# Products of zeros in PE's long waits, and the local layer's gate matmuls ahead of its first keys-major scores

## The chip, the cores and the metric

The kernel runs on one core of one Trainium2 chip. Its engines run side by side and meet at semaphores: TensorE (PE, matrix products into PSUM), VectorE (DVE), ScalarE (ACT), GpSimd (POOL) and SyncE (SP), which issues nearly all DMAs. The metric is the device time of one execution in microseconds (us). TensorE's clock is granted by the chip at 2.4 GHz or at 1.2 GHz; the profile shows it as PEclk, 1.00 or 0.50.

## The reference

Two transformer layers with adaptive layer norms over x of shape (2, 512, 256), all in float32:

```
mod = silu(c) @ wmod                       # sa, ca, ga, sb, cb, gb: shift, scale, gate, twice
ga, gb = sign * max(|.|, 0.25)
x = x + ga * attention(layernorm(x) * (1 + ca) + sa)
x = x + gb * ffn(layernorm(x) * (1 + cb) + sb)
```

Layer 0: sliding-window attention (16 heads of 16, a query sees itself and the 64 keys before it), then a mixture of 16 experts (4 chosen) and a shared expert. Layer 1: causal attention with 16 query heads and one key/value head, then a mixture of 8 experts (2 chosen) and a shared expert of width 1024. The gates and shifts of a layer come from `mod` and depend on c alone.

## The kernel before

Every engine has its own program, written out by hand in order; a semaphore wait holds everything behind it on that engine. Products in float32 precision are made of three or more products of high and low parts ("hi", "lo").

**Setup (L505 to 557).** PE computes the first shifts (`shifts(0, j, 7)`), then `norm_transposes(0)`: 16 transposes of the normalized x, for batch 0 from VectorE (`xn`, L1232), for batch 1 from ScalarE (L938).

**Maxima pass (`maxima_pass`, L653).** For each batch b and each of 16 heads PE computes scores in queries-major form (`scores`, L610) from a masked copy of q that ScalarE makes (`mask_q`, L959); VectorE reduces them to negated row maxima `nmx` (`maxima`, L1286). In layer 0 the projections of batch 1 (`project0(1, m)`) stand between the first four heads, and `max_rows(l, b)` (L644) transposes the maxima of a batch, which ScalarE and VectorE split into high and low parts (`max_high`, `max_low`). These are stored to DRAM, where they become two extra rows of q.

**Values pass (`values_pass`, L742).** SyncE loads q (with the maxima rows) and, in layer 0, k of each head from DRAM into four slots (`load_keys_major`, L309); a slot is refilled when its last reader, `keys_major(l, u)` (L679), has passed (`wait_ge(st, u - 3)`). `keys_major` computes the scores in keys-major form in two alternating halves of PSUM, ScalarE exponentiates them (`exponentials`, L1023, semaphore `p`; `keys_major` u waits for `p` u - 1), and after each four heads PE multiplies with V (`values`, L706); VectorE transposes and divides (`outputs`, L1309), GpSimd makes the low part (`out_low`, L431). In layer 0, between `keys_major` 1 and 2, PE computes the remaining shifts (`shifts_rest0`, 8 products of 2 columns) and the gates (`gates(0)`, 8 products of 256 columns in float32, two records each, into banks 6 and 7); PE then waits for the low maxima (`mlo`) and until ScalarE has copied the gates (`gate_taken`, L930), since the value products use the same banks. ScalarE does that copy behind its second exponential (L1043).

**Out-projection, norm, feed-forward.** `out_projection` (L774) ends PE's work of an attention. VectorE multiplies by the gate, adds to x, and takes the statistics (`gated`, L1360, `norm`, L1217), and PE waits for xn in `norm_transposes` (L541). ScalarE and VectorE make the modulated `hF` from the transposes (L946, L1242), PE zeroes the four output banks with `zero` (L812, products of `zeroR` with `maskR`, 512 columns), computes the router's `logits` (L782, 32 records of few columns), and goes into `ffn` (L818), whose first products wait for the high and low parts of h. Between the layers stand `shifts1` and `gates(1)`, then `norm_transposes(2)` and the projections of layer 1 (`project1`).

The functions that the diff touches:

Of the kernel before, what the change touches and what calls it, by code (L numbers as in the profile page):

```python
# [14 lines left out]
B, S, D = 2, 512, 256  # L15
# [46 lines left out]
def build(nc, io, out):  # L62
    ctx = ExitStack()
    with ctx:
# [24 lines left out]
        zeroR = sb("zeroR", [P, P], F32R)  # L89
# [390 lines left out]
        def _(pe):  # L480
# [126 lines left out]

            def scores(l, g, s, b):  # L610
                a = at[l]
                u = 4 * g + s
# [40 lines left out]
            def maxima_pass(l, beside):  # L653

                pe.wait_ge(consts, CONSTS)
                if l == 0:
                    pe.wait_ge(qlo, 4)
                else:
                    pe.wait_ge(v1_taken, 1)
                for b in range(B):  # L660

                    pe.wait_ge(qhi, (4, 6)[b] if l == 0 else 4 * B + 3 * (b + 1))
                    for s in range(SLOTS):
                        scores(l, BQ * b, s, b)
                        for work in beside[b][s]:
                            work()
                    if b:
                        if l:
                            pe.wait_ge(v1_taken, 2)
                        max_rows(l, 0)  # L670
                        if l == 0:
                            pe.wait_ge(qhi, 4 * B)
                    with pe.Fori(BQ * b + 1, BQ * (b + 1)) as g:
                        for s in range(SLOTS):
                            scores(l, g, s, b)
                max_rows(l, 1)


# [61 lines left out]
                        ins.then_inc(y_ps, 1)  # L740

            def values_pass(l):  # L742
                for s in range(2):
                    keys_major(l, s)
                if l == 0:
                    shifts_rest0()
                    gates(0)
                pe.wait_ge(at[l]["mlo"], B)
                if l == 0:
                    pe.wait_ge(gate_taken, 2)  # L750
# [23 lines left out]
            def out_projection(l):  # L774
# [3 lines left out]
                project_out(l, 1, range(OC - 1), False)  # L778
                pe.wait_ge(at[l]["ol"], QUADS)
                project_out(l, 1, range(OC - 1, OC), False)  # L780

            def logits(l):  # L782
                E = EXPERTS[l]
# [115 lines left out]
            ffn(0)  # L899
            shifts1()  # L900
            gates(1)
            norm_transposes(2)

            for m in range(4):
# [12 lines left out]
        def _(act):  # L917
# [119 lines left out]

            def attention(l):
                if l == 0:
                    act.wait_ge(split, 3)  # L1040
                for u in range(UNITS):
                    exponentials(l, u)
                    if l == 0 and u == 1:  # L1043
                        gates(0)

            attention(0)

# [570 lines left out]
```

## Time and profile before

| | us |
|---|---|
| median of 3 runs | 710.63 |
| the runs | 707.0, 710.63, 711.78 |
| the profiled execution | 715.33 |
| its span, first to last instruction | 713.5 |
| mean granted clock of TensorE | 0.955 |
| PE busy | 633.7 (89%) |
| VectorE busy | 389.9 (55%) |
| ScalarE busy | 294.0 (41%) |
| the chain that ended last: share of PE | 71% |
| the same: share of VectorE | 12% |

The times of all the views below are microseconds from the first instruction of that one execution. A timeline row merges like instructions: its start, its duration, engine, source line, operation, tiles and count, and in brackets how long the engine had been idle and who released it. The duration of a matrix product holds the tail of the last one, so the distance between starts is what one costs. A window row gives, for a stretch, the busy time of each engine with its number of instructions, then the granted clock. Work of PE in the two halves of a product in float32 shows as two records.

### The profile page before, as it was taken

How to read it: one execution, taken by the hardware profiler on the slowest of the kernel's cores; microseconds unless marked ns; L12 is line 12 of the kernel's file. 1: busy time of each engine (PE TensorE's matmuls, PEld its weight loads, DVE VectorE, ACT ScalarE, POOL GpSimd, SP SyncE). 2: the span in 40 equal slices, each digit the busy share in tenths (PEclk: the TensorE clock that was granted, in tenths of full speed). 3: DMA queues.
4: the chain of work that ended last, by engine and by line, in shares of the span. 5: the costliest groups of instructions: out<-in, count | busy, mean ns of one | idle time of the engine just before them, and what ended most of it. 6: DMA issues, size and time to landing. Idle time of an engine off the chain costs nothing.

```text
span 713.5 us, 11274 instructions
## 1 busy us (share of the span) xinstructions
PE 633.7 (89%) x3990; PEld 545.0 (76%) x3990; DVE 389.9 (55%) x730; ACT 294.0 (41%) x435; POOL 144.3 (20%) x142
## 2 busy tenths in 40 slices
PE   4989788859899999999999696779987799999995
PEld 3878677757788888888888575667667688888884
DVE  6378144676745544544457779952337633334455
ACT  4466255323443333343331743435660534433331
POOL 5411024403522222222220000001123032222220
PEclk9999799978999999999999999978999699999999
DMA  8444366310011111111100030412221001111101
GB/s 319 112 164 177 93 165 174 98 45 0 24 44 45 53 56 44 44 44 44 44 22 1 4 118 18 136 51 64 76 91 45 0 23 45 44 45 44 44 22 59
DMA packets 27199, 48.92 MB, mean 69 GB/s; under 512 B 4672, under 2 KB 9184, under 8 KB 27168
## 3 DMA queue, kind: packets, MB, share of 16 engines
q1 hardware_dynamic: 26848, 48.38, 22.1%
q8 instruction: 19, 0.31, 0.2%
q10 hardware_dynamic: 320, 0.13, 0.1%
q14 instruction: 12, 0.10, 0.0%
HBM read 36.57 MB, written 11.93 MB: 68 GB/s over the span
## 4 chain that ended last, share of the span: by engine, by line
PE 71%; DVE 12%; ACT 4%; SPq 4%; DMA 4%; issue 3%; POOL 1%; DVEq 0%; ACTq 0%
PE PS L492 33%; PE PS L831 15%; PE PS L700 3%; PE PS L723 3%; PE PS L736 3%; DVE nmx L1299 3%; PE PS L636 2%; DMA qk_slot<-k_scr 2%; PE PS L553 1%; SPq L318 1%; DVE stats L1207 1%; PE PS L789 1%; PE PS L702 1%; DVE xn L1369 1%; DVE x L1373 1%
## 5 line engine op out<-in xcount | busy, mean ns | idle before, releaser
L492 PE MATMUL PS<-h_hi,wqkv_hi 128*128 128x512 f32 x352 | 122.3, 407 | 4.0 <-POOL wqkv_hi L456 2.1
L1080 ACT ACTIVATE qk_hi<-xn 128x512 fp32r<-128x512 f32 x82 | 51.8, 632 | 178.0 <-DVE xn L1481 138.8
L492 PE MATMUL PS<-h_hi,wqkv_lo 128*128 128x512 f32 x336 | 113.7, 396 | 0.0
L1478 DVE TENSOR_TENSOR pr<-pr,PS 128x512 f32<-128x512 f32 x60 | 41.3, 688 | 86.8 <-PE PS L492 86.8
L492 PEld LDWEIGHTS PS<-h_hi,wqkv_hi 128*128 128x128 f32 x352 | 68.6, 195 | 19.4 <-POOL wqkv_hi L456 2.3
L1483 DVE TENSOR_TENSOR qk_lo<-xn,qk_hi 128x512 fp32r<-128x512 f32 x74 | 51.2, 692 | 52.7 <-ACT qk_hi L1080 52.7
L492 PE MATMUL PS<-h_lo,wqkv_hi 128*128 128x512 f32 x184 | 74.7, 406 | 0.0
L492 PEld LDWEIGHTS PS<-h_hi,wqkv_lo 128*128 128x128 f32 x336 | 63.5, 189 | 13.5 <-issue 0.3
L1076 ACT ACTIVATE pr<-PS 128x512 f32<-128x512 f32 x82 | 48.8, 596 | 43.0 <-PE PS L492 42.8
L831 PE MATMUL PS<-wqkv_hi,qk_hi 128*128 128x256 f32 x336 | 62.1, 284 | 3.3 <-POOL qk_lo L462 1.7
L456 POOL TENSOR_TENSOR wqkv_hi<-fw_raw,wqkv_hi 128x768 fp32r<-128x768 f32 x21 | 40.9, 1948 | 113.3 <-ACT wqkv_hi L1069 113.3
L492 PE MATMUL PS<-h_lo,wqkv_lo 128*128 128x512 f32 x160 | 62.8, 392 | 0.0
L456 POOL TENSOR_TENSOR wqkv_lo<-fw_raw,wqkv_lo 128x768 fp32r<-128x768 f32 x20 | 37.8, 1889 | 117.4 <-ACT wqkv_lo L1069 117.4
L831 PE MATMUL PS<-wqkv_lo,qk_hi 128*128 128x256 f32 x320 | 58.8, 283 | 1.6 <-DVE qk_lo L1483 1.5
L831 PEld LDWEIGHTS PS<-wqkv_hi,qk_hi 128*128 128x128 f32 x336 | 53.8, 188 | 8.3 <-POOL qk_lo L462 2.7
L1299 DVE TENSOR_REDUCE nmx<-PS 128x512 f32 (+4 forms) x96 | 53.8, 637 | 5.4 <-PE PS L639 5.3
L831 PEld LDWEIGHTS PS<-wqkv_lo,qk_hi 128*128 128x128 f32 x320 | 51.4, 188 | 5.5 <-DVE qk_lo L1483 1.7
L636 PE MATMUL PS<-qk_hi,q_masked 128*128 128x256 f32 (+2 forms) x128 | 40.0, 377 | 12.9 <-DVE nmx L1299 9.2
L963 ACT ACTIVATE q_masked<-qk_hi,headmask 128x512 fp32r (+1 forms) x64 | 43.1, 716 | 14.8 <-PE PS L639 12.5
L1314 DVE STREAM_TRANSPOSE o_parts<-PS 128x512 f32<-128x512 f32 x16 | 11.5, 717 | 67.7 <-PE PS L723 67.7
L831 PE MATMUL PS<-wqkv_hi,qk_lo 128*128 128x256 f32 x168 | 47.3, 281 | 0.0
L435 POOL TENSOR_TENSOR h_lo<-o_parts,h_hi 128x512 fp32r<-128x512 f32 x8 | 10.3, 1282 | 179.6 <-DVE h_hi L1327 179.6
(209 smaller groups left out, 1346.3 us busy)
## 6 DMA issues: line engine op xcount, KB each, us to landing
fw_raw<-in_ffn SPq DMA_DIRECT2D x41, 384.0 KB, 3.0
qk_slot<-q_scr SPq DMA_DIRECT2D x64, 132.0 KB
q_scr<-qk_hi SPq DMA_DIRECT2D x16, 256.0 KB
q_scr<-qk_lo SPq DMA_DIRECT2D x16, 256.0 KB
qk_slot<-k_scr SPq DMA_DIRECT2D x64, 64.0 KB
wmod<-in_wmod SPq DMA_DIRECT2D x1, 1536.0 KB, 13.4
x<-in_x SPq DMA_DIRECT2D x2, 512.0 KB, 4.2
wmod<-in_wmod SPq DMA_DIRECT2D x1, 1024.0 KB, 9.5
```

Of the source, the lines that this page charges most:

```text
L456: nc.gpsimd.tensor_tensor(fwR[s][1], fw[s][:, :], fwR[s][0].bitcast(F32), ALU.subtract)\
L492: ins = nc.tensor.matmul(dst, left(a, c), right(b, c), start=n == 0, stop=n == total - 1)
L636: nc.tensor.matmul(PS[:, bank, col:col + WIDTH1[qt]], qm[s][:, qt * P:(qt + 1) * P], qkR[0][:, 2, 0:WIDTH1[qt]], start=True, stop=True)
L700: nc.tensor.matmul(PS[:, bank, col:col + n], k1[:, b, kb * P:(kb + 1) * P], qk[s][:, kb * P:S], start=True, stop=True)
L723: ins = nc.tensor.matmul(PS[s * VW:(s + 1) * VW, O_BANK[g % 2], kb * P:kb * P + n], v, probs[l][slot][:, col:col + n], start=kb == 0, stop ...
L831: ins = nc.tensor.matmul(PS[:, 2 * b + t // 2, (t % 2) * D:(t % 2 + 1) * D], hidR[b][a][:, t * P:(t + 1) * P], fwR[s][w][:, 2 * D:], start ...
L963: nc.scalar.activation(qm[s][:, :], qkR[0][:, bass.ds(head // 2, 1), :].rearrange("p m t -> p (m t)").bitcast(F32), ACT.Copy, scale=headma ...
L1076: nc.scalar.activation(gact[b], PS[:, 4, :], ACT.Silu).then_inc(f["silu"], 1)
L1080: nc.scalar.activation(hidR[b][0], hid[b], ACT.Copy).then_inc(f["hi"], 1)
L1299: nc.vector.tensor_reduce(nmx[:, bass.ds(NT * u + qt, k)], PS[:, 3 * h + bank, 0:k * w].rearrange("p (t k) -> p t k", k=w), X, ALU.max, ne ...
L1478: tt(hid[b] if half is None else gu[b], gact[b], PS[:, 5, :], ALU.mult).then_inc(f["gu"], 1)
L1483: tt(hidR[b][1], hid[b], hidR[b][0].bitcast(F32), ALU.subtract).then_inc(f["lo"], 1)
```

## The change

It adds a helper that multiplies zeros into a PSUM bank that nothing reads, and calls it in seven places of PE's program: before the first scores of batch 1 in each layer (8 products in layer 0, 9 in layer 1, each behind a wait for the bank to be free), before the last `max_rows` of layer 1 (7), at the start of layer 1's values pass (10), at the end of each `out_projection` (30), and between `gates(1)` and `norm_transposes(2)` (7). In layer 0's values pass it moves `shifts_rest0` and `gates(0)` ahead of the first two `keys_major`, and on ScalarE it moves the copy of the gates ahead of the first exponential.

```diff
--- before.py
+++ after.py
@@ -607,6 +607,11 @@
 
 
 
+            def filler(count, bank):
+
+                for _ in range(count):
+                    nc.tensor.matmul(PS[:, bank, :], zeroR[:, :], maskR[:, 0:S], start=True, stop=True)
+
             def scores(l, g, s, b):
                 a = at[l]
                 u = 4 * g + s
@@ -659,6 +664,12 @@
                     pe.wait_ge(v1_taken, 1)
                 for b in range(B):
 
+                    if b and l == 0:
+                        pe.wait_ge(v_taken, 2)
+                        filler(8, 4)
+                    elif b:
+                        pe.wait_ge(qF_ready, 6)
+                        filler(9, 7)
                     pe.wait_ge(qhi, (4, 6)[b] if l == 0 else 4 * B + 3 * (b + 1))
                     for s in range(SLOTS):
                         scores(l, BQ * b, s, b)
@@ -673,6 +684,8 @@
                     with pe.Fori(BQ * b + 1, BQ * (b + 1)) as g:
                         for s in range(SLOTS):
                             scores(l, g, s, b)
+                if l:
+                    filler(7, 7)
                 max_rows(l, 1)
 
 
@@ -740,11 +753,13 @@
                         ins.then_inc(y_ps, 1)
 
             def values_pass(l):
-                for s in range(2):
-                    keys_major(l, s)
                 if l == 0:
                     shifts_rest0()
                     gates(0)
+                else:
+                    filler(10, 7)
+                for s in range(2):
+                    keys_major(l, s)
                 pe.wait_ge(at[l]["mlo"], B)
                 if l == 0:
                     pe.wait_ge(gate_taken, 2)
@@ -778,6 +793,7 @@
                 project_out(l, 1, range(OC - 1), False)
                 pe.wait_ge(at[l]["ol"], QUADS)
                 project_out(l, 1, range(OC - 1, OC), False)
+                filler(30, 7)
 
             def logits(l):
                 E = EXPERTS[l]
@@ -899,6 +915,7 @@
             ffn(0)
             shifts1()
             gates(1)
+            filler(7, 4)
             norm_transposes(2)
 
             for m in range(4):
@@ -1037,11 +1054,10 @@
 
             def attention(l):
                 if l == 0:
+                    gates(0)
                     act.wait_ge(split, 3)
                 for u in range(UNITS):
                     exponentials(l, u)
-                    if l == 0 and u == 1:
-                        gates(0)
 
             attention(0)
 
```

## Rows read from the trace of the kernel before

**Rows 1.** Waits of PE, whole span: us in total, times, longest us

```profile
PE PS L553 <- DVE xn L1232: 18.1, 3, 7.9
...
PE PS L636 <- ACT q_masked L963: 2.5, 1, 2.5
```

**Rows 2.** Timeline of PE, 155 to 165: start us, us, line [idle before <-releaser]

```profile
155.79 1.97 PE L553 MATMUL PS<-ident,xn 128*128 128x128 f32 x8 [7.89 <-DVE xn L1232]
...
159.12 2.05 PE L815 MATMUL PS<-maskR,zeroR 128*128 128x512 f32 x4
160.97 3.84 PE L789 MATMUL PS<-wg,hF 128*128 128x16 f32 x32
```

**Rows 3.** Timeline of PE, 376 to 430, between the layers

```profile
386.20 3.63 PE L500 MATMUL PS<-sc,wmod 128*128 128x2 f32 x32
389.70 5.39 PE L536 MATMUL PS<-wmod,hF 128*128 128x256 f32 x16
397.44 1.09 PE L553 MATMUL PS<-ident,xn 128*128 128x128 f32 x8 [2.36 <-DVE xn L1232]
```

**Rows 4.** Windows: length; PE, PEld, DVE, ACT, POOL busy; PEclk, DMA share, GB/s

```profile
52.30:55.60 3.30, 3.29 (x14) 3.30 (x15) 1.33 (x3) 2.79 (x5) 0.00 (x0) 0.50 0.49 138
76.10:86.30 10.20, 9.68 (x33) 8.78 (x34) 0.34 (x2) 2.90 (x3) 0.00 (x0) 0.50 0.38 99
151.20:161.20 10.00, 5.41 (x22) 5.02 (x23) 6.95 (x25) 4.54 (x8) 0.00 (x0) 0.50 0.01 2
472.10:485.50 13.40, 12.69 (x54) 10.92 (x56) 3.05 (x4) 8.60 (x7) 0.00 (x0) 0.50 0.21 59
554.00:560.60 6.60, 3.34 (x17) 3.34 (x17) 4.23 (x16) 2.56 (x5) 0.00 (x0) 0.50 0.00 0
560.80:564.00 3.20, 3.20 (x27) 3.02 (x26) 2.01 (x4) 3.15 (x6) 0.00 (x0) 1.00 0.00 0
```

**Rows 5.** Timeline of PE, 134 to 138, zero products at the high clock

```profile
137.19 0.63 PE L815 MATMUL PS<-maskR,zeroR 128*128 128x512 f32 x2
```

**Rows 6.** Timeline of PE, 46 to 62, batch change of the local maxima pass

```profile
52.31 0.66 PE L623 MATMUL PS<-maskR,identR 128*128 128x384 f32 x1 [2.04 <-ACT q_masked L963]
```

**Rows 7.** Timeline of PE, 464 to 492, start of the causal values pass

```profile
471.27 0.30 PE L650 MATMUL PS<-ident,nmx 128*64 128x128 f32 x1 [2.01 <-DVE nmx L1299]
...
484.09 1.07 PE L723 MATMUL PS<-pr,V 128*32 128x512 f32 x2
...
487.13 0.50 PE L700 MATMUL PS<-qk_slot,k 128*128 128x512 f32 x1
```

**Rows 8.** Timeline of PE, 70 to 98, start of the local values pass

```profile
75.06 0.44 PE L691 MATMUL PS<-maskR,identR 128*128 128x384 f32 x1 [1.05 <-DMA qk_slot<-k_scr]
...
78.23 3.46 PE L500 MATMUL PS<-sc,wmod 128*128 128x2 f32 x16
81.55 6.04 PE L536 MATMUL PS<-wmod,hF 128*128 128x256 f32 x16
88.81 0.41 PE L691 MATMUL PS<-maskR,identR 128*128 128x384 f32 x1 [1.22 <-issue]
...
95.61 0.44 PE L691 MATMUL PS<-maskR,identR 128*128 128x384 f32 x1 [0.68 <-DMA qk_slot<-k_scr]
```

**Rows 9.** Timeline of ScalarE, 66 to 95

```profile
76.18 1.28 ACT L1030 ACT_TABLE_LOAD   x1 [1.86 <-PE PS L692]
77.47 0.81 ACT L1030 ACTIVATE pr<-PS 128x768 f32<-128x768 f32 x1
...
87.62 1.08 ACT L930 ACTIVATE gate<-PS 128x512 f32<-128x512 f32 x2 [8.35 <-PE PS L536]
```

**Rows 10.** Timeline of ScalarE, 144 to 176

```profile
159.91 1.43 ACT L946 ACTIVATE hF<-PS,modT 128x512 f32<-128x512 f32 x2
```

**Rows 11.** Timeline of ScalarE, 464 to 492

```profile
473.14 1.28 ACT L1036 ACT_TABLE_LOAD   x1 [1.27 <-DVE mxT_lo L1306]
474.44 2.37 ACT L1036 ACTIVATE pr<-PS 128x1280 f32<-128x1280 f32 x2
```

## The prediction

> **What bounds the kernel now.** I read the waits of TensorE (PE) first. Its largest wait by far is for the normalized x: 18.1 us in three waits, the longest 7.9 [rows 1]. The first of them takes 7.89 us [rows 2], the one between the layers 2.36 [rows 3], which leaves 7.9 for the last. I then cut the granted clock into stretches [rows 4]. Around each long wait the clock falls from 2.4 to 1.2 GHz (1.00 to 0.50) and stays low well into the work that follows: 3.3 us after the batch change of the first maxima pass, 10.2 us at the start of the local values pass, 10.0 us around the first of the long normalization waits, 13.4 us at the start of the causal values pass, 6.6 us around the last. PE carries 9.7 us of records in the second stretch and 12.7 in the fourth, so there the low clock costs time on the path; in the third only 5.4 of 10.0 us are work. The timelines of PE and ScalarE (ACT) then tell which of this work ends last [rows 5 to 11].
>
> **The price of a filler.** Four products of zeros of this shape (128x512) take from 159.12 to 160.97, 0.46 us each at the low clock [rows 2]; half of it, 0.235 with rounding up, is the price at the high one, where two of them last 0.63 with the tail of the second [rows 5]. The diff's counts come to 8 x 0.235 = 1.9 us, 9: 2.1, 7: 1.6, 10: 2.35, 30: 7.05. The waits they stand in are 2.04 (8, first maxima pass, [rows 6]), 2.5 (9, [rows 1]), 2.01 (7 before the last row of maxima, [rows 7]), 2.36 (7 before the third normalization, [rows 3]) and 7.89 and 7.9 (30 each). All but the ten fit, with 0.1 to 0.9 us to spare, and cost nothing. If the cover were gone each would cost its whole length; at the low clock the 30 would take 13.8 us. Do zeros hold the clock? The clock is low through 3.3 us of transposes and rises at 161.2, right behind the four zero products of 159.12 [rows 2, 4]. I take it that they count.
>
> **Part by part.** The sum is made in the profiled execution (715.33 us, span 713.5).
>
> (a) Eight fillers in the local maxima pass. PE works at 1.2 GHz from 52.31 to 55.6 [rows 4, 6]; at 2.4 that is 1.6 us less. But ScalarE is busy 2.79 of these 3.30 us, with the masks and the q and k parts that PE and VectorE need next, and behind them VectorE's reductions set the pace; I take 0.45, near the lower end. Ends: 0 and 1.6.
>
> (b) The moved shifts and gates. Now: PE comes free at 74.0, waits 1.05 us for the first query/key slot, does two keys-major scores, then shifts (3.3 us) and gates (6.0), ends at 87.6 and starts the third score at 88.8 [rows 8]. After: shifts start at 74.0. In the second layer the same kind of chain runs without a wait before it: 32 shift records in 3.50 us at 2.4 GHz, and 16 gate records in 5.39, in which the clock is low for a part [rows 3]. So 16 x 0.11 = 1.75 and 5.2: gates end at G = 74.0 + 6.95 = 80.95, 6.65 us earlier. Ends: gates all at 2.4 (3.4 us), or shifts 3.46 and gates 6.8, all at 1.2 (G = 84.3). What follows G gets later, since it loses what it did before. ScalarE copies the gates (1.08), waits for the first score (G + 1.1), loads its exponential table (1.28) and takes 0.81 us for each exponential [rows 9]: the third score starts at G + 3.3 and the fourth at G + 4.15, where before it was G + 1.2. SyncE, which had refilled slots 0 and 1 in the shadow of the gates, now issues these loads after the first scores, so two of the pass's 28 refills fall into it. A slot's refill takes 5.0 us: the fourth score ended at 90.6 (88.81 plus two scores of 0.9) and the same slot's next started at 95.61, waiting for a DMA [rows 8]. So that score now starts at G + 5.1 + 5.0 = G + 10.1 = 91.05, not 95.61: 4.5 us gained. From there on the pass repeats. VectorE's shift copy and gate steps come earlier too, ahead of its first output block, and nobody waits for them; GpSimd's queue has nothing in it. Ends: 1.2 (G = 84.3) to 6.2.
>
> (c) Thirty fillers behind the first out-projection. At 2.4 GHz eight transposes take 0.93 us instead of 1.77 [rows 2, 3]. From 155.79: transposes to 157.65, zeros to 158.6, first half of the logits (16 x 0.115; 32 take 3.84 with a tail) to 160.4; the second half waits for ScalarE's hF, which will end 0.95 earlier than its 161.34 [rows 10], so also at 160.4; with a tail of 0.15 they end at 162.35 instead of 164.81 [rows 2], 2.5 us. The logits are tiny products and the clock can fall within them, as it now does right behind them; 0.3 off: 2.2. The router's VectorE chain starts from there and all moves along. Ends: 0.9 (hF's gain alone) and 3.5.
>
> (d) The same 30 in the second layer, the same working: 2.2.
>
> (e) Seven fillers before the third normalization, nine at the batch change of the second maxima pass: the clock is high in both places as it is. 0.
>
> (f) Causal values pass. Seven fillers keep the clock up over the 2.01 us wait. Ten more delay the first score from 471.4 to 473.75, and with it the table load, which waits for that score (473.14 now, [rows 11]): load at 474.95, first exponential to 477.45, third score at 477.6. From then one score per exponential (1.2 us each, [rows 11]), the sixth ends at 482.5. The value products last from 484.09 to 487.13 with the rise at 485.5 [rows 4, 7]: 1.6 us at the high clock and 1.4 at the low, so 2.3 all at the high. The next score starts at 484.85 instead of 487.13. Gain 2.3. Where an execution of before had not fallen here, the ten fillers cost 1.9 instead.
>
> Sum: 0.45 + 4.5 + 2.2 + 2.2 + 2.3 = 11.65, the profiled execution would take 703.7. It lies 4.7 us above the median (710.63) and the three runs spread over 4.8. The chance falls of the clock, (a) and (f), can be such a spread: I give (f) only 0.8 against the median, the odds of 6 to 4 between 2.3 and -1.9 rounded up a little. 710.6 - 10.1 = **700.5 us**.
>
> **Rivals.**
> 1. The clock still falls in the causal pass. With the fillers there is now a gap of 1.6 us between the second and third score, where ScalarE loads its table. If it falls there, or if it mostly had not fallen before, (f) is -1.9: 703.2 us. For it: a fall at 472 behind 2 us of idling. Chance 0.15.
> 2. Transposes do not hold the clock. After the 30 fillers a rest of 0.8 us and 1.9 us of transposes follow; if the clock falls there, zeros and logits run at 1.2 and (c) and (d) keep 0.9 each: 703.1 us. Against it: in the last normalization the clock rose at 560.7, right behind 3.3 us that held hardly anything but transposes [rows 4]. Chance 0.08. The Trainium skill, page "TensorE: Matmul & The Clock Gate", section "Part 4: PE-mode transpose", says that transposes do not count as busy for the clock; by that rule this rival would be the forecast, and the trace speaks against it.
> 3. The moved gates run all at 1.2 GHz, behind shifts that give the clock no reason to stay up, and the refills pile up: (b) 1.2, total 703.8 us. Chance 0.10.
> 4. Zeros do not hold the clock: slower. It falls 3.3 us into each 30 as it does now [rows 2, 4], the other 16 take 0.46, and PE is 10.7 us behind the out-projection free instead of 7.9: 2.8 us late, twice. In the causal pass two fillers take 0.235, eight 0.46, and the first exponential comes 4.3 us late. 5.6 + 4.3 - 4.5 of (b) = 5.4 us slower, 716.0 us. The point from which it is slower than before: (b) gains under 9.9 us, which its rows exclude to exceed; only the first assumption decides. Against it: the rise behind the zeros [rows 2, 4]. Chance 0.05.
> The moved code is certain to run; that it does not do what it says has no chance of its own.
>
> **How the numbers follow.** Forecast 0.55, own range 696 to 704. Rivals 0.38, and 0.07 for mixtures of small losses, 704 to 709. The range that leaves out 2 in 10 is 695.5 to 707. A measurement of this kernel tells 1% (7.1 us) from no change: faster means under 703.5. That is most of the forecast (0.51), half of rivals 1 and 2 (0.12) and 0.04 of rival 3, some 0.68 in all; slower by 1% (over 717.7) is the upper half of rival 4, 0.03, and a tail of mishaps, 0.02; the rest, 0.27, is within 1%.
>
> **What would show it.** Clock at 1.00 from the first out-projection's end through the transposes, and 8 of them in 0.93 us; third local score 2 us or more behind the gates; gates in about 5.2 us; first causal exponential near 2 us later than now against the last maxima, but the seventh score 2.3 earlier; fillers ending ahead of the event they wait with. Wrong would be: a clock of 0.50 within the fillers, or refill waits on the first eight slots that grow beyond 5 us.

## The result and the profile after

The changed kernel takes **702.51 us** in the median of 15 runs (699.03 to 707.37), the kernel before on the same chip 710.95 in 15 runs (707.0 to 715.1). The ratio is **0.9898, 95% interval 0.9874 to 0.9922**: 7.3 us less by the ratio (5.5 to 9.0), 8.4 by the medians, where 10.1 were forecast. The forecast of 700.5 is 2.0 us too low, inside its range. The mean granted clock of TensorE in the profiled executions rises from 0.955 to 0.983.

The profiled execution of the changed kernel took 702.60 us, that of before 715.33. That difference, 12.7, is not the change's worth: 715.33 lies above all the 15 runs that the kernel before was given beside the changed one. The head of the page after:

```profile
span 700.8 us, 11475 instructions
...
PE 642.4 (92%) x4091; PEld 550.0 (78%) x4091; DVE 390.1 (56%) x730; ACT 293.7 (42%) x435; POOL 144.3 (21%) x142
```

PE is busy for 8.7 us more, in a span that is 12.7 shorter, because the records of the zeros count as busy. VectorE, ScalarE and GpSimd do what they did. Next the waits of PE (us in total, times, longest). The wait for `xn` that led the list [rows 1] is down from 18.1 us to 2.5: the zeros now stand in it.

```profile
PE PS L553 <- DVE xn L1248: 2.5, 3, 0.9
```

Windows of the changed kernel, columns as in [rows 4], whose stretches they answer: the batch change of the first maxima pass, the start of the local values pass, the first normalization, the logits behind it, the start of the causal values pass, the second long normalization.

```profile
50.20:55.60 5.40, 5.25 (x34) 4.46 (x33) 3.42 (x7) 5.14 (x10) 0.00 (x0) 1.00 0.33 92
75.80:79.00 3.20, 3.20 (x9) 2.55 (x8) 0.05 (x1) 0.00 (x0) 0.00 (x0) 0.50 0.54 161
143.30:157.40 14.10, 13.20 (x80) 11.02 (x79) 11.18 (x37) 5.71 (x10) 0.00 (x0) 1.00 0.00 0
157.80:161.00 3.20, 3.20 (x10) 2.62 (x10) 2.17 (x9) 1.59 (x2) 0.00 (x0) 0.50 0.00 0
464.80:477.20 12.40, 11.76 (x92) 9.38 (x92) 3.24 (x4) 8.65 (x8) 0.00 (x0) 1.00 0.25 73
539.40:553.40 14.00, 13.10 (x79) 10.92 (x78) 11.07 (x37) 5.94 (x11) 0.00 (x0) 1.00 0.01 2
```

The clock is at 2.4 GHz in four of the six, and each of the four holds work that was at 1.2 before. In the local values pass it still falls, for 3.4 us where it had been 10.2.

### The profile page after: what moved, and what is told of

It reads as the page before. It is cut to its first block, busy times and chain, and to the rows that moved or that the text cites. A ratio compares the mean times of both kernels' runs of the same rounds, so it can differ in the third digit from the quotient of the medians.

```text
span 700.8 us, 11475 instructions
## 1 busy us (share of the span) xinstructions
PE 642.4 (92%) x4091; PEld 550.0 (78%) x4091; DVE 390.1 (56%) x730; ACT 293.7 (42%) x435; POOL 144.3 (21%) x142
## 4 chain that ended last, share of the span: by engine, by line
PE 73%; DVE 13%; ACT 6%; DMA 3%; issue 3%; POOL 1%; SPq 1%; DVEq 0%; ACTq 0%
PE PS L492 33%; PE PS L847 16%; PE PS L736 4%; PE PS L749 3%; DVE nmx L1315 3%; PE PS L713 3%; PE PS L641 2%; PE PS L628 2%; DMA qk_slot<-k_scr 2%; PE PS L630 1%; PE PS L704 1%; ACT q_masked L980 1%; DMA w_raw<-in_wqkv 1%; DVE x L1389 1%; DVE xn L1385 1%
## 5 line engine op out<-in xcount | busy, mean ns | idle before, releaser
L492 PE MATMUL PS<-h_hi,wqkv_hi 128*128 128x512 f32 x352 | 121.8, 405 | 4.0 <-POOL wqkv_hi L456 2.1
L492 PE MATMUL PS<-h_hi,wqkv_lo 128*128 128x512 f32 x336 | 113.6, 396 | 0.0
L492 PEld LDWEIGHTS PS<-h_hi,wqkv_hi 128*128 128x128 f32 x352 | 67.9, 193 | 19.2 <-POOL wqkv_hi L456 2.3
L492 PEld LDWEIGHTS PS<-h_hi,wqkv_lo 128*128 128x128 f32 x336 | 63.4, 189 | 13.4 <-issue 0.3
L492 PE MATMUL PS<-h_lo,wqkv_hi 128*128 128x512 f32 x184 | 73.7, 400 | 0.0
L492 PE MATMUL PS<-h_lo,wqkv_lo 128*128 128x512 f32 x160 | 62.8, 393 | 0.0
```

Of the source, the lines that this page charges most:

```text
L492: ins = nc.tensor.matmul(dst, left(a, c), right(b, c), start=n == 0, stop=n == total - 1)
```

## Where the time went, stretch by stretch

The table gives the time between starts of PE's rows in one profiled execution of each kernel, in us. "Maxima row" is the transposition of the last maxima of a pass (L650 before, L655 after), "T" the transposes of a long normalization, "ffn" the first product of the feed-forward (L492), "down" its first down product. The kernels below "changed" are those of the experiments.

| kernel | start to local maxima row | to 3rd score | to 8th score | maxima row to T 1 | T 1 to ffn | ffn to T 2 | causal maxima row to 7th score | T 3 to ffn | ffn to down |
|---|---|---|---|---|---|---|---|---|---|
| before | 73.71 | 15.10 | 21.90 | 82.08 | 8.87 | 232.78 | 15.86 | 8.82 | 8.19 |
| changed | 73.43 | 10.65 | 17.68 | 77.98 | 6.71 | 232.78 | 12.38 | 6.80 | 7.29 |
| changed, second profile | 73.09 | 10.66 | 17.42 | 79.42 | 6.56 | 234.26 | 12.39 | 6.56 | 7.54 |
| only the new order | 73.88 | 10.65 | 16.66 | 75.88 | 8.76 | 232.75 | 11.89 | 8.81 | 8.15 |
| only the zeros | 73.50 | 14.94 | 21.77 | 79.78 | 6.56 | 234.26 | 12.39 | 6.57 | 7.55 |
| changed without the ten | 71.76 | 10.66 | 17.81 | 78.37 | 7.04 | 234.86 | 15.90 | 6.56 | 7.54 |
| changed without the thirties | 73.69 | 10.65 | 17.81 | 75.35 | 8.91 | 232.78 | 12.37 | 8.80 | 8.24 |
| only the thirties | 75.21 | 10.46 | 17.74 | 77.45 | 7.74 | 232.75 | 15.87 | 6.57 | 7.54 |
| new order and thirties | 74.13 | 10.65 | 16.94 | 76.82 | 6.56 | 234.26 | 11.97 | 6.56 | 7.53 |
| narrow zeros | 75.02 | 12.32 | 19.40 | 84.22 | 9.02 | 232.78 | 12.39 | 8.82 | 8.28 |
| eight behind the scores | 75.00 | 12.29 | 19.11 | 77.76 | 6.56 | 234.25 | 11.87 | 6.56 | 7.55 |
| gates between | 73.48 | 10.02 | 17.18 | 75.67 | 7.64 | 232.86 | 12.38 | 7.61 | 8.03 |
| combined | 72.31 | 9.47 | 16.29 | 74.31 | 6.86 | 234.28 | 10.59 | 6.57 | 7.54 |
| combined, second profile | 75.04 | 9.32 | 16.51 | 75.25 | 7.74 | 232.80 | 10.59 | 6.56 | 7.54 |

From before to changed the stretches that don't overlap give 0.3 (start), 4.1 (local values pass), 2.2 (T 1 to ffn), 3.5 (causal values pass), 2.0 and 0.9 (around the second router): 13.0 of gains, against 12.7 in the spans; the rest of the passes takes 0.2 back. Most columns take only a few distinct values, with the clock falling or not and with how long it stays low. Much of what separates two executions of one kernel goes with that, and not all: in the 15 runs of the changed kernel, those with a mean clock of 0.986 took 699.0 to 700.7 and those with 0.974 to 0.976 took 704.8 to 706.5, but the longest, 707.37, had 0.981. So one trace tells the mechanism, and the timed runs tell the worth.

## The experiments

All compute the whole reference. The ratio is each kernel's to the kernel before on the same chip. The changed kernel was compared by itself (before: mean 710.9); e1 to e4, e6 to e9 and g1 to g4 each shared a chip and its runs of before (means 711.7, 710.2 and 711.6 us). Behind ± stands the standard error of the mean.

| kernel | median us | mean us | ratio, 95% interval |
|---|---|---|---|
| changed | 702.51 | 702.90 ± 0.66 | 0.9898, 0.9874 to 0.9922 |
| e1 only the new order | 708.97 | 709.27 ± 0.73 | 0.9997, 0.9959 to 1.0035 |
| e2 only the zeros | 704.08 | 704.57 ± 0.53 | 0.9924, 0.9894 to 0.9954 |
| e3 changed without the ten | 705.86 | 705.48 ± 0.72 | 0.9949, 0.9915 to 0.9983 |
| e4 changed without the thirties | 706.99 | 707.12 ± 0.60 | 0.9970, 0.9936 to 1.0004 |
| e6 narrow zeros | 722.4 | one run | |
| e7 eight behind the scores | 703.61 | 703.53 ± 0.50 | 0.9921, 0.9888 to 0.9953 |
| e8 gates between | 701.43 | 701.48 ± 0.47 | 0.9903, 0.9865 to 0.9942 |
| e9 combined | 701.13 | 700.21 ± 0.84 | 0.9903, 0.9866 to 0.9939 |
| g1 changed again | 701.25 | 702.14 ± 1.18 | 0.9856, 0.9813 to 0.9899 |
| g2 only the thirties | 708.33 | 706.95 ± 0.96 | 0.9933, 0.9895 to 0.9970 |
| g3 new order and thirties | 703.95 | 704.05 ± 0.68 | 0.9893, 0.9855 to 0.9931 |
| g4 combined again | 699.53 | 699.89 ± 0.64 | 0.9833, 0.9795 to 0.9870 |

Two kernels stand in the table twice. The changed one has 0.9898 and 0.9856, the combined one 0.9903 and 0.9833: the same kernel differs by 3 and by 5 us from one chip to the next. Differences of 2 or 3 us between kernels of different chips are within that scatter.

### The two halves of the change

**Only the new order** (all calls of `filler` taken out of the changed kernel):

```diff
-                filler(30, 7)
...
-            filler(7, 4)
...
                 if l == 0:
                     shifts_rest0()
                     gates(0)
-                else:
-                    filler(10, 7)
```

> Only the moved shifts and gates, none of the zero products. Theory (my sum, (b)): gates end about 6.9 us behind the last maxima row instead of 13.9, and 4.5 us are gained against before: ratio 0.9937, 706.5 us. The two long normalization waits are as before, with a granted clock of 0.50 at the transposes (8 in 1.77 us). Rival (refills eat it, or gates all at 1.2 GHz): 1.2 us gained, ratio 0.998. Rival (the order does it all): 7.3 us, ratio 0.990.

**Only the zeros** (the order of before on PE and ScalarE, all calls of `filler` kept):

```diff
-                if l == 0:
-                    shifts_rest0()
-                    gates(0)
-                else:
+                if l:
                     filler(10, 7)
                 for s in range(2):
                     keys_major(l, s)
+                if l == 0:
+                    shifts_rest0()
+                    gates(0)
```

> All the zero products, but shifts and gates where they were. Theory: what the order does not give, some 4 us at the two normalizations (2.2 each) and 0 to 3.5 in the causal pass, depending on whether an execution of before had fallen there: in all 4 to 5 us, ratio 0.994. Rival (zeros are worth nothing in the median, the profiled execution of before was only an unlucky one): ratio 1.00. Rival (they do it all): 0.990.

The zeros alone give most of it, 0.9924. The order alone can't be told from nothing by its ratio; by the means on that chip it is 2.4 us faster. Yet its trace shows third and eighth score as early as in the changed kernel (10.65 and 16.66 behind the maxima row), 4.5 and 5.2 us ahead of the profiled execution of before. The mechanism is there and most of the time isn't. Either the pass takes back later what it gained, or the execution of before with which they are compared was an unlucky one.

### The groups of zeros

**Without the ten** (the `filler(10, 7)` at the start of the causal values pass taken out):

```diff
                 if l == 0:
                     shifts_rest0()
                     gates(0)
-                else:
-                    filler(10, 7)
```

> The changed kernel without the ten zero products at the start of the causal values pass. Theory A (my (f)): ScalarE's table load waits for the first score, so the ten cost 1.9 us wherever the clock would not have fallen: this kernel is up to 1.9 us faster than the changed one when the clock stays up, and 2 to 3.5 slower when it falls. Theory B (from the changed kernel's trace): the load stands behind the DMA issues at 466.65, so the first exponential comes only 0.5 us earlier than in the changed kernel, and the idle gap between second and third score grows to about 2.1 us; time within 1 us of the changed kernel's where the clock holds.

**Without the thirties:**

```diff
                 project_out(l, 1, range(OC - 1, OC), False)
-                filler(30, 7)
```

> The changed kernel without the two times thirty zero products. Theory: loses 2.2 us at each of the two long normalizations, 4.4 us slower than the changed kernel, near 707 us, ratio to before 0.995; the clock is at 0.50 at the transposes, 8 of them in 1.77 us, and the first product of the feed-forward stands 8.9 us behind the end of the wait as before, where the changed kernel has 6.7. Rival (the wait of the transposes or hF sets the pace, whatever the clock): no loss, ratio 0.990.

Without the ten the kernel is 2.6 us slower than the changed one by the means, 3.6 by the ratios, and 1.9 if each mean is first taken against the mean of before on its own chip; the intervals of the two ratios overlap. Its trace shows where the time goes. PE's rows at the start of the causal values pass, without the ten:

```profile
465.87 0.30 PE L655 MATMUL PS<-ident,nmx 128*64 128x128 f32 x1 [0.33 <-DVE nmx L1313]
...
470.42 0.76 PE L713 MATMUL PS<-qk_slot,k 128*128 128x512 f32 x1 [2.11 <-ACT pr L1051]
...
481.77 0.50 PE L713 MATMUL PS<-qk_slot,k 128*128 128x512 f32 x1
```

The same of the changed kernel:

```profile
462.60 1.84 PE L613 MATMUL PS<-maskR,zeroR 128*128 128x512 f32 x7
464.77 0.30 PE L655 MATMUL PS<-ident,nmx 128*64 128x128 f32 x1 [0.33 <-DVE nmx L1315]
464.83 2.57 PE L613 MATMUL PS<-maskR,zeroR 128*128 128x512 f32 x10
467.24 0.39 PE L713 MATMUL PS<-qk_slot,k 128*128 128x512 f32 x1
...
469.84 0.48 PE L713 MATMUL PS<-qk_slot,k 128*128 128x512 f32 x1 [0.34 <-ACT pr L1053]
...
477.15 0.50 PE L713 MATMUL PS<-qk_slot,k 128*128 128x512 f32 x1
```

The ten take the place of the wait between the second and the third score: 0.34 us of it are left instead of 2.11. With the wait the clock fell and the seventh score came 15.90 us behind the maxima row; with the zeros 12.38. In the five traces without the ten it fell every time, but not alike. In three (before, this one, only the thirties) it stayed low for 10.2 to 13.7 us, and the seventh score came at 15.86 to 15.90. In two (only the new order, new order and thirties) it fell 0.1 us behind the maxima row or less and was back after 3.4 us, ahead of the third score; there the seventh came at 11.89 and 11.97. Windows of the kernel with only the new order, whose maxima row stands at 465.36:

```profile
465.50:468.50 3.00, 3.00 (x12) 2.81 (x12) 2.43 (x4) 1.50 (x2) 0.00 (x0) 0.50 0.11 30
469.00:475.00 6.00, 5.16 (x40) 4.67 (x42) 0.31 (x1) 5.35 (x5) 0.00 (x0) 1.00 0.30 86
```

Four of the five, all but this one, also lack the seven zeros ahead of the maxima row, and in those four the fall begins within 0.8 us of that row. In the seven traces with ten or eight zeros there it never fell.

Without the thirties 4.2 us are lost by the means and 5.1 by the ratios, and 3.5 by means taken against before on each chip; T 1 to ffn and T 3 to ffn are back at 8.91 and 8.80.

### Do busy records hold the clock?

**Narrow zeros.** Each 30 of 512 columns become 90 of 32 columns.

```diff
-                filler(30, 7)
+                for _ in range(90):
+                    nc.tensor.matmul(PS[:, 7, 0:32], zeroR[:, :], maskR[:, 0:32], start=True, stop=True)
```

> The changed kernel with each run of 30 products of 512 columns replaced by 90 products of zeros of 32 columns, about the same time of busy instructions (PE near 6 us busy at 2.4 GHz). Theory (columns streamed hold the clock, not instructions): the clock falls to 0.50 within or behind them, transposes again take 1.77 us per 8, and the first feed-forward product comes 8.8 us behind the transposes instead of 6.7. Rival (any PE instruction holds it): clock 1.00 through the transposes, 6.7 us.

PE's rows and two windows of this kernel:

```profile
143.95 15.45 PE L797 MATMUL PS<-maskR,zeroR 128*128 128x32 f32 x90
159.24 1.97 PE L553 MATMUL PS<-ident,xn 128*128 128x128 f32 x8
```

```profile
144.00:147.50 3.50, 3.50 (x34) 3.50 (x33) 3.43 (x12) 0.00 (x0) 0.00 (x0) 1.00 0.00 0
148.20:158.00 9.80, 9.80 (x48) 9.80 (x47) 3.35 (x17) 2.08 (x4) 0.00 (x0) 0.50 0.00 0
```

PE is busy for every microsecond of both windows, and the clock falls all the same. At the high clock 34 records take 3.5 us (0.10 each), at the low one 48 take 9.8 (0.20). Even at 0.10 each the ninety would have taken 9.3 us, not the 6 that had been expected, and so more than their cover of 7.9. At the low clock they outgrew it by far: the transposes start 15.3 us behind the first of them, and run at the low clock too, 1.97 us for eight. The second layer does the same, and this single run took 722.4 us. Thirty products of 512 columns over 7.2 us held the clock, ninety of 32 columns did not. An engine that is shown busy is not by that alone one that keeps its clock.

### The place of the zeros in the causal pass

**Eight behind the first two scores** instead of ten ahead of them:

```diff
-                else:
-                    filler(10, 7)
                 for s in range(2):
                     keys_major(l, s)
+                if l:
+                    filler(8, 7)
```

> Changed kernel, but in the causal pass 8 zero products behind the first two scores instead of 10 ahead of them. Theory B (the table load does not wait for the first score): from the last maxima row to the seventh score 11.9 us instead of 12.4, as the kernel with the order alone showed by luck; the clock stays at 1.00 in every execution; median 0.5 us under the changed kernel, ratio 0.989. Theory A (it waits): 1.9 us faster. Rival: the clock falls all the same (the wait before the last row ends it): 15.9 us and a ratio near 0.994.

ScalarE in this kernel, and then in the changed one:

```profile
469.26 1.28 ACT L1053 ACT_TABLE_LOAD   x1 [1.27 <-DVE mxT_lo L1322]
470.56 2.37 ACT L1053 ACTIVATE pr<-PS 128x1280 f32<-128x1280 f32 x2
```

```profile
466.02 0.59 ACTq L256 DMA_DIRECT2D q_scr<-mxT_lo  x1
466.65 1.28 ACT L1053 ACT_TABLE_LOAD   x1 [1.27 <-DVE mxT_lo L1322]
468.46 2.37 ACT L1053 ACTIVATE pr<-PS 128x1280 f32<-128x1280 f32 x2 [0.53 <-PE PS L715]
```

The maxima rows start at 467.38 and 464.77, so the load comes 1.88 us behind both, though the first score stands 0.11 behind the maxima row in the one and 2.47 in the other. In the changed kernel the load even starts before the first score does (467.24). It stands behind ScalarE's DMA issues, not behind the score. In the local pass it is otherwise: the load of before starts at 76.18, when the first score has ended at 76.10 [rows 8, 9], and in the kernel with the gates between, whose first score ends at 76.64, ScalarE stands idle between the DMA issue and the load:

```profile
74.78 0.60 ACTq L256 DMA_DIRECT2D q_scr<-mxT_lo  x1
76.72 1.28 ACT L1048 ACT_TABLE_LOAD   x1 [2.62 <-PE PS L705]
```

In the local program two waits stand ahead of that exponential, in the causal one a single one; no run tests whether this decides it. In the causal pass ten zeros ahead of the scores therefore delay the first exponential by 0.5 us only (3.69 against 3.18 behind the maxima row), which the seventh score shows too, 12.38 against 11.87. The timed runs don't tell the two places apart: 0.9921 against 0.9898, intervals overlapping.

### The order by itself, against the thirties

**Only the thirties** is the kernel before with a `filler(30, 7)` at the end of `out_projection` and nothing else:

```diff
                 project_out(l, 1, range(OC - 1, OC), False)
+                filler(30, 7)
```

> The kernel before with nothing but the two times thirty zero products. Theory: 2.2 us at each of the two long waits (8.8 to 6.6 from transposes to the feed-forward's first product), plus 0.7 behind the second (8.2 to 7.5), less what a fall of the clock near 181 us takes back (1.5): 3.5 to 5 us, ratio 0.994. Rival (the order does more than the zeros): under 2 us, 0.998.

**New order and thirties** is the changed kernel without the small groups:

```diff
-                    if b and l == 0:
-                        pe.wait_ge(v_taken, 2)
-                        filler(8, 4)
-                    elif b:
-                        pe.wait_ge(qF_ready, 6)
-                        filler(9, 7)
...
-                if l:
-                    filler(7, 7)
...
-                else:
-                    filler(10, 7)
...
-            filler(7, 4)
```

> Moved shifts and gates with the two times thirty, none of the 8, 9, 7, 10, 7. Against the run with the thirties alone it shows the order, against the changed kernel the small groups. Theory X (the traces): the order gives 4 us, as the stretch from the last local maxima row to the transposes is 77 us where it was 81; ratio 0.988, and the small groups nothing but the causal 1 to 2. Theory Y (the medians so far): the order gives 2, the small groups 2.5 us, ratio 0.992: the DMA-bound pass takes back what was gained up to the eighth score.

**Changed again**, unaltered, for the same chip:

> The changed kernel once more, on the chip of the three below. Ratio to before 0.988 to 0.990; the reference for the other three.

By the ratios: the thirties alone 4.8 us, the order on top of them 2.8, the small groups on top of both 2.6; by the means of this chip 4.7, 2.9 and 1.9. The first is clear of the noise. For the order and for the small groups the intervals of the ratios overlap. The changed kernel itself came out at 0.9856, better than the 0.988 to 0.990 expected of it. The old order's local values pass, in the kernel with only the thirties (PE, then two windows):

```profile
75.21 0.30 PE L655 MATMUL PS<-ident,nmx 128*64 128x128 f32 x1 [1.22 <-DVE nmx L1299]
...
77.34 1.86 PE L500 MATMUL PS<-sc,wmod 128*128 128x2 f32 x16
79.07 5.39 PE L536 MATMUL PS<-wmod,hF 128*128 128x256 f32 x16
85.67 0.42 PE L696 MATMUL PS<-maskR,identR 128*128 128x384 f32 x1 [1.22 <-issue]
...
92.95 0.45 PE L696 MATMUL PS<-maskR,identR 128*128 128x384 f32 x1 [1.15 <-DMA qk_slot<-k_scr]
```

```profile
75.30:78.90 3.60, 3.43 (x28) 3.26 (x28) 0.28 (x1) 1.96 (x3) 0.00 (x0) 1.00 0.78 191
79.10:82.30 3.20, 3.20 (x9) 2.57 (x10) 0.34 (x2) 0.90 (x2) 0.00 (x0) 0.54 0.49 116
```

These rows show that the old order is not always late. Here it had its shifts at the high clock (1.86 us where [rows 8] have 3.46) and a low stretch of 3.4 us, not 10.2; its first two scores also waited only 0.2 us for their slots, where those of before waited 1.6 and those with only the zeros 1.3. Its third score comes 10.46 us behind the maxima row and its eighth 17.74, as early as in the new order. The 15.10 and 21.90 of the profiled execution of before, which came up again with only the zeros (14.94, 21.77), are the old order with a low stretch of 10.2 us. The new order has a bad draw too, 12.3 and 19.1 to 19.4 in two of its traces, but a smaller one.

The table gives the order's worth once more, by averages over traces. From the maxima row to T 1 the three traces of the old order take 79.8 us and seven of the new one (the narrow zeros left out, which delay T 1 themselves) 77.4, which is 2.4 less. From the eighth score to T 1 it is 59.3 and 59.7. So little of the gain is taken back later, and most of the forecast's excess comes from the one execution of before.

### A version with both repaired

**Gates between**: the shifts stay ahead, the first two scores come next, then the gates; ScalarE copies them behind its second exponential as before.

```diff
                 if l == 0:
                     shifts_rest0()
-                    gates(0)
                 else:
                     filler(10, 7)
                 for s in range(2):
                     keys_major(l, s)
+                if l == 0:
+                    gates(0)
```

> Changed kernel with the local layer's order: shifts, first two scores, gates, third score; ScalarE's gate copy behind its second exponential as before. Theory (the moved gates keep two refills and two exponentials out of their shadow, and the pass lives on its DMAs, so a part of the 4.2 us gained up to the eighth score is given back): the third score starts as early as in the changed kernel (10.5 us behind the last maxima row), the eighth 16.7 to 17.2 us behind it instead of 17.7, and the whole stretch to the transposes is 1 to 2 us shorter; ratio 0.987. Rival (refills are hidden by latency anyway): same as the changed kernel, 0.990. Rival (scores at 1.2 GHz and the gates all at it): 1 us slower.

The third score came 10.02 us behind the maxima row, the eighth 17.18 and T 1 75.67, where seven traces of the new order have 77.4 on average: as the theory had it, in one trace. The timed runs don't confirm it. The ratio is 0.9903, where 0.987 was expected and the changed kernel has 0.9898 and 0.9856. Some of it went elsewhere, at least in the trace: behind both long waits the clock was low for 6.8 us, and T to ffn took 7.64 and 7.61.

**Combined**: the shifts go ahead of the last local maxima row, into a wait of 1.2 us; the gates stand between the second and third score; in the causal pass two zeros stand behind the first two scores, and ScalarE makes its exponential table load early, with an exponential of a tile of two columns, ahead of the last split of the maxima.

```diff
                 if l:
                     filler(7, 7)
+                else:
+                    shifts_rest0()
                 max_rows(l, 1)
...
             mask_rest(1, 1)
+            nc.scalar.activation(bqs[:, :], bqs[:, :], ACT.Exp).then_inc(act_order, 1)
             max_high(1, 1)
...
-                if l == 0:
-                    shifts_rest0()
-                    gates(0)
-                else:
-                    filler(10, 7)
                 for s in range(2):
                     keys_major(l, s)
+                if l == 0:
+                    gates(0)
+                else:
+                    filler(2, 7)
```

> The version the readings point to: shifts_rest0 ahead of the last maxima row of the local layer (in a wait of 1.22 us), first two scores, then gates as in the run before; in the causal pass the exponential table is loaded by an exponential of two columns ahead of the last maxima row, and two zero products behind the first two scores instead of ten ahead. The other zero products stay. Theory: 0.8 us from the shifts, 1 to 2 from the order, 1.8 in the causal pass: 3.5 to 4.5 us under the changed kernel, ratio 0.984. Rival (the DMA-bound local pass takes back what is gained before it): only the causal 1.8, 0.987. Rival (too few zeros in the causal pass, the clock falls): 0.990.

Its trace has the earliest scores of all (9.47 and 16.29 behind the maxima row, the seventh causal one 10.59), and the clock held in the causal pass with two zeros. The ratio, 0.9903, is no better than the changed kernel's, and 0.984 had been expected; the mean, 700.21, is 2.7 us under that of the changed kernel, which ran on another chip.

And the same kernel once more, beside the changed one:

> The combined version once more, beside the changed kernel on one chip. Theory: 2.5 to 3.5 us under it (its trace: 1.8 in the causal pass, 1.1 ahead of the gates, 0.4 to the transposes), ratio 0.985. Rival: no difference that can be measured, 0.989.

The start of the local values pass in that second run of it, and ScalarE at the start of its causal pass:

```profile
73.31 1.86 PE L500 MATMUL PS<-sc,wmod 128*128 128x2 f32 x16
75.04 0.28 PE L655 MATMUL PS<-ident,nmx 128*64 128x128 f32 x1
...
78.62 4.52 PE L536 MATMUL PS<-wmod,hF 128*128 128x256 f32 x16
84.36 0.41 PE L706 MATMUL PS<-maskR,identR 128*128 128x384 f32 x1 [1.22 <-issue]
...
91.55 0.45 PE L706 MATMUL PS<-maskR,identR 128*128 128x384 f32 x1 [1.07 <-DMA qk_slot<-k_scr]
```

```profile
465.05 0.60 ACTq L256 DMA_DIRECT2D q_scr<-mxT_lo  x1
465.70 2.37 ACT L1054 ACTIVATE pr<-PS 128x1280 f32<-128x1280 f32 x2 [1.28 <-PE PS L717]
```

The exponential stands right behind the DMA issues with no table load between, and the seventh causal score comes 10.59 us behind the maxima row instead of 12.38; third and eighth local score come 1.3 and 0.9 us earlier than in the changed kernel run beside it (its maxima row stands behind the shifts, which puts up to 0.5 us of them into the first column). Together that is 2 to 3 us in the traces. The clock gives part of it back elsewhere (T 1 to ffn 7.74 against 6.56 there). The timed runs show 0.9833 against 0.9856 on the same chip, with overlapping intervals. It has the lowest mean of its chip in both comparisons and beats the kernel before clearly; that it beats the changed one is likely by the traces and not shown by the times.

## Why the prediction was right, and which of its terms were not

**Zeros hold the clock: right.** PE's rows behind the first out-projection of the changed kernel:

```profile
143.35 7.16 PE L613 MATMUL PS<-maskR,zeroR 128*128 128x512 f32 x30
151.41 1.09 PE L553 MATMUL PS<-ident,xn 128*128 128x128 f32 x8 [0.90 <-DVE xn L1248]
...
154.22 4.06 PE L805 MATMUL PS<-wg,hF 128*128 128x16 f32 x32
158.12 0.77 PE L492 MATMUL PS<-h_hi,wqkv_hi 128*128 128x512 f32 x1
```

Thirty take 7.16 us with a tail, 0.239 each against the 0.235 of the sum, and eight transposes 0.93 as worked out; the clock is 1.00 from 143.3 to 157.4. Rival 4, the slower outcome, has fallen.

**(c) and (d), the thirties: right.** 2.2 each were forecast; T 1 to ffn is 2.16 shorter and T 3 to ffn 2.02. The timed runs give 3.5 to 5.1 us for both, against 4.4. There is a detail that the step named as a risk: the clock falls again in the logits or right behind them (157.7 here). Where it kept up through the logits, T to ffn is 6.56, another 0.15 to 0.24 less. In some traces it also falls later, in the feed-forward. Two windows around that point, in the kernel with only the zeros:

```profile
160.00:181.00 21.00, 16.59 (x84) 12.91 (x84) 17.53 (x24) 7.10 (x11) 11.67 (x4) 1.00 0.00 1
181.60:184.80 3.20, 3.20 (x8) 2.53 (x9) 2.59 (x7) 0.38 (x1) 1.07 (x1) 0.50 0.41 123
```

Behind a wait of 2.11 us for GpSimd's high parts of the weights the clock falls for 3.4 us, and ffn to T 2 takes 234.26 instead of 232.78. The changed kernel has that wait too (2.13, at 179.83 in the trace shown) and had no fall there. So 1.5 us of the first layer's gain are given back in some executions: the four traces with 6.56 all have 234.25 or 234.26. An earlier fall does not rule out the later one. Without the ten, the clock was low in the logits and again behind that wait, and ffn to T 2 took 234.86:

```profile
155.90:162.50 6.60, 6.60 (x22) 5.44 (x22) 4.74 (x17) 2.19 (x3) 0.00 (x0) 0.51 0.00 0
180.00:183.00 3.00, 3.00 (x9) 2.32 (x8) 2.09 (x7) 0.60 (x1) 0.57 (x1) 0.50 0.41 131
```

The wait is in all fourteen traces, the fall behind it in six: in the three that had no fall between T 1 and it, and in three (this one, new order and thirties, the first combined one) that had. In the second layer there is no such wait, and instead ffn to down came 0.65 to 0.90 earlier, which no step had counted.

**(b), the moved gates: the mechanism right, the term mis-sized.** The step said: gates end at G = 6.95 us behind the point where PE comes free, third score at G + 3.3, eighth at 91.05. The trace:

```profile
73.43 0.30 PE L655 MATMUL PS<-ident,nmx 128*64 128x128 f32 x1 [1.22 <-DVE nmx L1309]
73.56 1.88 PE L500 MATMUL PS<-sc,wmod 128*128 128x2 f32 x16
75.31 5.39 PE L536 MATMUL PS<-wmod,hF 128*128 128x256 f32 x16
80.34 0.53 PE L704 MATMUL PS<-maskR,identR 128*128 128x384 f32 x1
...
84.08 0.41 PE L704 MATMUL PS<-maskR,identR 128*128 128x384 f32 x1 [1.81 <-ACT pr L1047]
...
91.11 0.44 PE L704 MATMUL PS<-maskR,identR 128*128 128x384 f32 x1 [0.91 <-DMA qk_slot<-k_scr]
```

ScalarE copies the gates at 80.73, loads its table at 81.83 and begins the exponentials at 83.13, [rows 9] with the order turned round. Gates to 80.34, 6.8 behind 73.56; third score at G + 3.7; eighth at 91.11, 10.8 behind G. Every event came within 0.7 us of the step, and the refill is again what the eighth score waits for (0.91). But the term, 4.5, was a difference against one execution of before, and that had a low stretch of 10.2 us. The runs give 0.2 (order alone), 1.9 (changed against only the zeros) and 2.8 us (on top of the thirties) by the ratios, and 2.4, 0.9 and 2.9 by means taken against before on each chip: about 2 in the middle, with no single one well clear of the noise. The traces, averaged, give 2.4. The step had called only the falls in (a) and (f) a matter of chance, though (b) rests on one as much. That is the step that failed. The pass behind it scatters as well: from the eighth score to T 1 it took between 57.5 and 62.0 us (64.8 with the narrow zeros), with no relation to the order.

**(f), the causal pass: a premise wrong, a term too small.** The step held the table load to be waiting for the first score, as it does in the local pass (76.18 against 76.10). Here it doesn't (466.65 against the first score's 467.24). So the ten delay the first exponential by 0.5 us and not 1.9; against an execution with a long fall the gain is 3.5 us and not 2.3, and against one with a short early fall it is -0.5. An execution without the ten and without a fall, which the step priced at -1.9, is in no trace. With a long fall in three of five traces without the ten, an estimate is 0.6 x 3.5 - 0.4 x 0.5 = 1.9 us, where 0.8 had been counted. The runs: 1.9 to 3.6 for the ten alone, 1.9 to 2.6 for all small groups together. Rival 1 priced this term at -1.9: its gap of 1.6 us between the second and third score is 0.34, and the clock held in all traces with the ten.

**(a) and (e): small, as said.** With the eight zeros the clock is 1.00 at the first batch change in the trace above (the first of the windows), and they end at 52.28, 0.15 ahead of the scores that follow. Those start at 52.43 where they started at 52.31 [rows 6], so the eight fill their wait to the end and leave nothing to spare.

From the start to the last local maxima row it is 73.62 us in the mean over eight traces with them (71.76 to 75.02; the two combined ones left out, which have shifts in it) and 74.23 over four without (73.71 to 75.21): 0.6 us within a scatter of 3, against 0.45 forecast, and so neither shown nor contradicted.

**Rivals 2 and 3.** Rival 3 had the moved gates all at 1.2 GHz; the low stretch in them is 3.4 us in most traces and 6.8 in two, and the third score was 12.3 behind the maxima row at the worst. Its price, 1.2 for (b), is nevertheless nearer to what the order is worth than the 4.5, for another reason. Rival 2 had the clock fall in the transposes: in the changed kernel, from 151.41 to 153.1, it is 1.00. The Trainium skill, page "TensorE: Matmul & The Clock Gate", section "Part 4: PE-mode transpose", has it that transposes don't count as busy. The thirty zeros just ahead may have carried the clock over these 1.7 us, so this trace doesn't test the rule; it shows that it did no harm here. In the kernel before, the clock rose at 560.7 behind transposes that began at 557.26 and little else, which speaks against the rule for these.

**The sum with measured terms.** Thirties 3.5 to 5.1, order about 2, small groups 1.9 to 2.6: 7.4 to 9.7 us, beside 7.3 (ratio) and 8.4 (medians) for the whole. The forecast's 4.4 + 4.5 + 1.25 had the middle term too large by about 2.5 and the last too small by about 1. The errors partly cancel, so that the total came within 2.0 us is in part luck.

**Open.** Whether the order is worth 1 us or 3, and why the clock falls in the logits in one execution and in the feed-forward in the next; the traces show which, not what decides it. That the small groups give more than the ten alone isn't shown either, nor what decides whether a table load waits for the score.

## What to carry to other kernels

Where TensorE waits for some microseconds ahead of a dense stretch and the granted clock falls there, products of zeros of full width (512 columns here), sized to end just before the event, buy back the low stretch: here 2 us for each wait of 8. Before a low stretch is put into a sum as a gain, ask whether it comes with every execution; where the falls are chance, count the mean over executions and not the one that was profiled. And a filler can also close a wait that it does not fill: ten zeros ahead of two scores closed the 2 us wait behind them, at a price of 0.5 us.

## What the hardware did that I had not expected

- Ninety products of 32 columns kept PE at 100% of records and did not keep the clock: it fell to 0.50 within 5 us (148.2), and one took 0.20 us where it had taken 0.10.
- In the causal pass ScalarE's table load (1.28 us) ran ahead of the wait of the exponential that needs it, right behind the DMA issue before it (466.65, with the first score's start at 467.24). In the local pass it came only when the first score had ended (76.18 after 76.10 in the kernel before, 76.72 after 76.64 with the gates between). With the table loaded earlier by an exponential of two columns, the first exponential of the pass stood right behind the DMA issues (465.70).
- Behind a 2.1 us wait for GpSimd in the feed-forward the clock fell in six of fourteen traces (at 181.6 us with only the zeros), three of which had lost it in the logits or just behind them too, and ffn to T 2 was 1.5 to 2.1 us longer in these six than in the kernel before.
